# First norm with tokens as rows, x in four transfers, weight products moved behind the router product

## The reference

```python
x = x + 0.5 * L0_ffn(layernorm(x), Wg, W_in, W_out)   # 8 experts, top 2 with capacity, gelu(a) * g
x = x + L0_attn(layernorm(x), ...)                    # 16 heads of 8, causal, ALiBi
x = x + 0.5 * L0_ffn(layernorm(x), ...)
x = x + 0.5 * L1_ffn(x, ...)                          # latent attention, rope, 8 experts + shared
x = x + L1_attn(x, ...)                               # convolution, scan, feed-forward
x = x + 0.5 * L1_ffn(x, ...)
```

## Time and profile before

| | us |
|---|---|
| median of 3 runs | 1422.37 (1421.27 to 1424.42) |
| the profiled execution | 1424.82 |
| its span, first to last instruction | 1423.0 |
| TensorE busy | 1323.8 (93%) |
| VectorE busy | 1005.4 (71%) |
| ScalarE busy | 871.2 (61%) |
| GpSimdE busy | 400.2 (28%) |
| mean granted TensorE clock | 0.981 |

### The profile page before, as it was taken

One profiled execution on the slowest core, in us unless ns is written; L12 is line 12 of the kernel. 1 busy time (PEld: TensorE's weight loads), 2 busy tenths in 40 slices (PEclk: granted clock), 3 DMA queues, 4 the chain that ended last, 5 costly groups with the idle time before them and its releaser, 6 DMA issues.

```text
span 1423.0 us, 27091 instructions
## 1 busy us (share of the span) xinstructions
PE 1323.8 (93%) x10934; PEld 562.0 (39%) x10934; DVE 1005.4 (71%) x1516; ACT 871.2 (61%) x1104; POOL 400.2 (28%) x331
## 2 busy tenths in 40 slices
PE   7999998889879999999999998989998999999997
PEld 5344333333324444333444343433433334433443
DVE  3534777889925347698887868688868697978735
ACT  3334347788784454276566767666768676675672
POOL 5554430110011755452220223022305033202010
PEclk8999999999999999999999999999999999999998
DMA  6633101000001731011111010110010101100100
GB/s 177 118 62 70 25 14 31 16 2 2 2 1 39 196 60 34 1 32 24 35 24 24 1 23 1 24 35 10 15 24 1 23 13 24 31 13 19 24 1 15
DMA packets 30291, 45.80 MB, mean 32 GB/s; under 512 B 5892, under 2 KB 10692, under 8 KB 30116
## 3 DMA queue, kind: packets, MB, share of 16 engines
q1 hardware_dynamic: 30168, 44.08, 14.0%
HBM read 25.39 MB, written 1.18 MB: 19 GB/s over the span
## 4 chain that ended last, share of the span: by engine, by line
PE 72%; DVE 11%; ACT 8%; issue 4%; SPq 3%; DMA 2%; POOL 0%; ACTq 0%; DVEq 0%
PE ps L1264 13%; PE ps L1364 11%; PE ps L1309 7%; ACT PR L1442 6%; PE ps L1230 5%; PE ps L1250 5%; PE ps L1231 5%; PE ps L1232 5%; DVE BM L1530 3%; PE ps L1844 3%; PE ps L1328 2%; PE ps L1242 2%; PE ps L1271 2%; PE ps L1375 2%; PE ps L1324 1%
## 5 line engine op out<-in xcount | busy, mean ns | idle before, releaser
L1442 ACT ACTIVATE PR<-ps 128x1024 f32<-128x1024 f32 x432 | 431.2, 1026 | 207.1 <-PE ps L1271 136.4
L1530 DVE TENSOR_REDUCE BM<-ps 128x2 f32<-128x1024 f32 (+2 forms) x384 | 350.4, 950 | 57.0 <-PE ps L1250 55.9
L1264 PE MATMUL ps<-QS,KS 48*128 48x512 f16 (+7 forms) x2688 | 306.1, 329 | 31.7 <-ACT PR L1442 22.5
L1364 PE MATMUL ps<-PR,VS 128*32 128x512 f32 (+3 forms) x2304 | 231.5, 499 | 2.2 <-ACT PR L1442 1.6
L1264 PEld LDWEIGHTS ps<-QS,KS 48*128 48x128 f16 (+1 forms) x2688 | 108.5, 95 | 203.6 <-ACT PR L1442 88.5
L1250 PE MATMUL ps<-KS,QS 48*128 48x128 f16 (+2 forms) x1728 | 161.7, 273 | 19.2 <-DVE BM L1530 10.8
L1523 DVE TENSOR_REDUCE BM<-ps 128x8 f32<-128x1024 f32 x96 | 116.8, 1220 | 39.3 <-PE ps L1250 38.5
L1250 PEld LDWEIGHTS ps<-KS,QS 48*128 48x128 f16 x1728 | 68.0, 94 | 135.3 <-issue 45.8
L1571 POOL TENSOR_TENSOR OS<-OS,RX 128x512 f32<-128x512 f32 x24 | 30.5, 1270 | 273.9 <-ACT RX L1458 273.9
L1230 PE MATMUL ps<-YA,QS 128*128 128x512 f16 x256 | 99.6, 389 | 0.8 <-DVE RX L1489 0.5
L1231 PE MATMUL ps<-YA,QS 128*128 128x512 f16 x256 | 99.2, 388 | 0.0
(11 more groups left out here) (299 smaller groups left out, 2054.9 us busy)
## 6 DMA issues: line engine op xcount, KB each, us to landing
PR<-gates SPq DMA_DIRECT2D x32, 512.0 KB, 12.5
QS<-KS SPq DMA_DIRECT2D x64, 128.0 KB
QS<-KS SPq DMA_DIRECT2D x64, 64.0 KB
WM<-W_in SPq DMA_DIRECT2D x1, 2048.0 KB, 9.0
QS<-HL SPq DMA_DIRECT2D x48, 32.0 KB
KS<-HL SPq DMA_DIRECT2D x48, 32.0 KB
QS<-CT SPq DMA_DIRECT2D x96, 2.0 KB
KS<-KS SPq DMA_DIRECT2D x8, 128.0 KB, 2.4
```

The costliest lines, as they stand in the source:

```text
L1264: ins = pe.matmul(ps[pair][:, w, off:off + cols], KS[rows, ks, kt * P:(kt + 1) * P], QS[rows, qs, (ph + 1) * TT - cols:(ph + 1) * TT], sta ...
L1364: ins = pe.matmul(dst[32 * j:32 * j + 32, TT - cols:TT], v, PR[:, buf, j, off:off + cols], start=(g == 0), stop=(g == NGRP[ph] - 1))
L1442: act.activation(dst, src, ACT.Exp, scale=0.125 if lat else 1.0).then_inc(sig["exp"], 1)
L1530: ins = dve.tensor_reduce(BM[:, ph, p, :, qt - 4 * ph, part], bnk[:, :, off:off + nk * P], AX.X, ALU.max)
```

## The change

x comes in four transfers of a quarter each, with a semaphore each, again token-major (`XR`). VectorE takes bn_stats and bn_aggr of each row (a token) and normalises with one tensor_scalar per 128 tokens, with mean and 1/std as scalars of the partition (`XS`). ScalarE computes 1/std for 4 x 128 tokens in one instruction of 128x4. TensorE turns x and the normalised rows, 16 tiles each; ScalarE copies both out of PSUM. The weight products leave the hand-written start and become two planner tasks `cmp` 0 and 1 on TensorE behind `rlg`, with priority 0. W_in and W_out are asked for earlier, only W_in is waited for before the experts begin, and the wait for all small weights moves from the front of TensorE's plan to the first down matmul.

```diff
-            "scl": 0.75, ... "cmc": 0.6}
+            "scl": 0.75, ... "cmc": 0.6, "cmp": 2.6}
...
-        if kind in ("rlg", "rrk", "rtp"):
+        if kind in ("rlg", "rrk", "rtp", "cmp"):
             return 0
...
-            x = add("DVE", "eh", ("eh", u), x, ("ed", u - self.NHE) if u >= self.NHE else None)
+            x = add("DVE", "eh", ("eh", u), x, ("ed", u - self.NHE) if u >= self.NHE else self.staged(u))
...
         self.router()
         for i in range(2):
-            self.add("ACT", "cm", ("cmc", i))
+            self.add("ACT", "cm", ("cmc", i), self.add("PE", "cm", ("cmp", i), ("rlg",)))
...
+    def staged(self, u):
+        return ("cmp", 1) if u >= 4 else None
...
-            sp.dma_start(PRf[:, 0:T].rearrange("p (i d) -> p i d", i=NTT),
-                         a["x"].rearrange("(i p) d -> p i d", p=P)).then_inc(s_x0, 16)
+            for t in range(NT):
+                sp.dma_start(XR[:, t, :, :], a["x"].rearrange("(t i p) d -> t p i d", p=P, t=NT)[t]).then_inc(s_x[t], 16)
             for dst, src in ((wqn, a["wqn"]), (wkb, a["wkb"]), (won[0], a["won"][:, 0:H // 2]),
-                             (won[1], a["won"][:, H // 2:H])):
+                             (won[1], a["won"][:, H // 2:H]), (w_rt0[:, :], a["Wg0"])):
                 sp.dma_start(dst, src).then_inc(s_wc, 16)
+            sp.dma_start(w_in, a["W_in"].rearrange("e p f -> p e f")).then_inc(s_wm, 16)
             loads = [
-                (w_rt0[:, :], a["Wg0"]), (wq0[:, :, :], ...),
+                (w_out, a["W_out"].rearrange("e (c p) o -> p e c o", p=P)), (wq0[:, :, :], ...),
...
-            load_moe_weights(sp)
...
         def pe_load(pe):
             pe.wait_ge(s_const, 1)
+            for t in range(NT):
+                pe.wait_ge(s_x[t], 16)
+                for i in range(4):
+                    ins = pe.transpose(bank(t)[:, i * P:(i + 1) * P], XR[:, t, i, :], identf[:, :])
+                ins.then_inc(s_ld, 1)
+            for t in range(NT):
+                pe.wait_ge(s_xc, t + 1)
+                pe.wait_ge(s_xup, t + 1)
+                for i in range(4):
+                    ins = pe.transpose(bank(t)[:, i * P:(i + 1) * P], XS[:, t, i, :], identf[:, :])
+                ins.then_inc(s_ld, 1)
 
         def dve_load(dve):
+            def stats(t):
+                dve.wait_ge(s_x[t], 16)
+                for i in range(4):
+                    ins = dve.bn_stats(STAT[:, t, i, :], XR[:, t, i, :])
+                ins.then_inc(s_mean, 1)
+                dve.wait_ge(s_mean, t + 1)
+                for i in range(4):
+                    ins = dve.bn_aggr(MV[:, t, i, :], STAT[:, t, i, :])
+                ins.then_inc(s_var, 1)
+            stats(0)
             for t in range(NT):
+                if t + 1 < NT:
+                    stats(t + 1)
+                dve.wait_ge(s_var, t + 1)
                 dve.wait_ge(s_rs, t + 1)
+                for i in range(4):
+                    ins = dve.tensor_scalar(XS[:, t, i, :], XR[:, t, i, :], MV[:, t, i, 0:1], RSTD[:, t, i:i + 1],
+                                            ALU.subtract, ALU.mult)
+                ins.then_inc(s_xc, 1)
+
+        def act_load(act):
             act.preload_act_table_set(LN_EXP)
+            act.wait_ge(s_const, 1)
             for t in range(NT):
                 act.wait_ge(s_var, t + 1)
+                act.activation(RSTD[:, t, :], MV[:, t, :, 1], ACT.Ln, bias=epsc[:, 0:1]).then_inc(s_va, 1)
+                act.wait_ge(s_va, t + 1)
+                act.activation(RSTD[:, t, :], RSTD[:, t, :], ACT.Exp, scale=-0.5).then_inc(s_rs, 1)
+                act.wait_ge(s_ld, t + 1)
+                act.copy(XT[:, tsl(t)], bank(t)).then_inc(s_xup, 1)
             for t in range(NT):
+                act.wait_ge(s_ld, NT + t + 1)
+                act.copy(XN[:, tsl(t)], bank(t)).then_inc(s_xn, 1)
...
             if kind == "rlg":
+                if not lat:
+                    pe.wait_ge(s_wc, 80)
...
                 if u >= plan.NHE:
                     dve.wait_ge(sig["ed"], c("ed", u - plan.NHE))
+                elif not lat and u >= 4:
+                    dve.wait_ge(sig["cmp"], 2)
...
+                elif kind == "cmp":
+                    i, = args
+                    for h in range(H):
+                        g, j = divmod(h, QUAD)
+                        if i == 0:
+                            ins = pe.matmul(bank(4)[:, h * 32:(h + 1) * 32], wqn[:, h, :], wkb[:, h, :], start=True, stop=True)
+                        else:
+                            ins = pe.matmul(bank(5)[32 * j:32 * j + 32, g * P:(g + 1) * P], wkb[:, h, :],
+                                            won[h // 8][:, h % 8, :], start=True, stop=True)
+                    ins.then_inc(sig["cmp"], 1)
                 else:
+                    if task == ("ed", 0):
+                        pe.wait_ge(s_w, N_WFIRST)
                     pe_attn(pe, False, c, plan, task)
...
-            act.wait_ge(s_wm, 32)
...
+                if task == ("ewh", 0):
+                    act.wait_ge(s_wm, 16)
...
             plan, c = plan_of(False), counter(False)
-            dve.wait_ge(s_wm, 32)
+            dve.wait_ge(s_wm, 16)
...
             pe_load(pe)
-            pe_norm(pe)
-            pe.wait_ge(s_w, N_WFIRST)
+            pe.wait_ge(s_const, N_CONST)
             pe_first(pe)
```

More of the change, by code:

```diff
@@ L321, in weights_ready @@
     def weights_ready(self, u):
+        return None
+    def staged(self, u):
         return None
@@ L779, in pr_part @@
             return PRf[:, o:o + n]
-        NSQ = pr_part(0, 2048).rearrange("p (a t) -> p a t", a=NT)
-        NRS = pr_part(2048, 2048).rearrange("p (a t) -> p a t", a=NT)
+        XR, XS = (pr_part(i * T, T).rearrange("p (t i d) -> p t i d", t=NT, i=4) for i in range(2))
+        STAT = pr_part(2 * T, 96).rearrange("p (t i c) -> p t i c", t=NT, i=4)
+        MV = pr_part(2 * T + 96, 32).rearrange("p (t i c) -> p t i c", t=NT, i=4)
+        RSTD = pr_part(2 * T + 128, 16).rearrange("p (t i) -> p t i", t=NT)
         GB = pr_part(0, 8192).rearrange("p (a e t) -> p a e t", a=2, e=E)
@@ L826, in build_program @@
         gate_d = nc.dram_tensor("gates", (4, E, T), F32, kind="Internal").ap()
-        s_x0 = sem("s_x0")
+        s_x = [sem(f"s_x{t}") for t in range(NT)]
         s_w = sem("s_w")
@@ L919, in pool_const @@
             ch.up(pool.memset(pick[:, :], 0.0))
+            ch.up(pool.memset(epsc[:, 0:1], EPS))
             ch.wait()
@@ L946, in pool_const @@
                 ins = pool.memset(desc[:, e:e + 1], float(E - e))
-            pool.memset(epsc[:, 0:1], EPS)
             ins = pool.memset(epsc[:, 1:2], EPS * EPS)
@@ L952, in pe_load @@
             pe.wait_ge(s_const, 1)
-            pe.wait_ge(s_x0, 16)
-            for i in range(NTT):
-                ins = pe.transpose(bank(i // 4)[:, (i % 4) * P:(i % 4 + 1) * P],
-                                   PRf[:, i * P:(i + 1) * P], identf[:, :])
-                if i % 4 == 3:
-                    ins.then_inc(s_ld, 1)
-        def dve_load(dve):
-            for t in range(NT):
-                dve.wait_ge(s_ld, t + 1)
-                dve.tensor_copy(XT[:, t * TT:(t + 1) * TT], bank(t)).then_inc(s_xup, 1)
@@ L973, in pe_comp @@
-        def pe_comp(pe, heads):
-            pe.wait_ge(s_wc, 64)
-            for h in heads:
-                ins = pe.matmul(bank(4)[:, h * 32:(h + 1) * 32], wqn[:, h, :], wkb[:, h, :], start=True, stop=True)
-            if h == H - 1:
-                ins.then_inc(s_comp, 1)
-        def pe_comp_out(pe):
-            for h in range(H):
-                g, j = divmod(h, QUAD)
-                ins = pe.matmul(bank(5)[32 * j:32 * j + 32, g * P:(g + 1) * P], wkb[:, h, :], won[h // 8][:, h % 8, :],
-                                start=True, stop=True)
-            ins.then_inc(s_comp, 1)
@@ L989, in pe_norm @@
-        def pe_norm(pe):
-            pe_comp(pe, range(0, 4))
-            pe.wait_ge(s_const, N_CONST)
-            pe.wait_ge(s_xup, NT)
-            for t in range(NT):
-                pe.matmul(bank(t), mean_w[:, :], XT[:, tsl(t)], start=True, stop=True).then_inc(s_mean, 1)
-            pe_comp(pe, range(4, 12))
-            for t in range(NT):
-                pe.wait_ge(s_sq, t + 1)
-                pe.matmul(bank(t), mean_w[:, :], NSQ[:, t, :], start=True, stop=True).then_inc(s_var, 1)
-            pe_comp(pe, range(12, H))
-            pe_comp_out(pe)
@@ L1002, in dve_norm @@
-        def dve_norm(dve):
-            for t in range(NT):
-                dve.wait_ge(s_mean, t + 1)
-                dve.tensor_tensor(XN[:, tsl(t)], XT[:, tsl(t)], bank(t), ALU.subtract).then_inc(s_xc, 1)
-            for t in range(NT):
-                dve.wait_ge(s_rs, t + 1)
-                dve.tensor_tensor(XN[:, tsl(t)], XN[:, tsl(t)], NRS[:, t, :], ALU.mult).then_inc(s_xn, 1)
-        def act_norm(act):
+            for t in range(NT):
[3 more added lines that the diff above has]
+                ins.then_inc(s_ld, 1)
```

(10 more changed lines are left out.)

20 lines of the change are left out of this document (7 added, 13 removed).

## The result

The changed kernel took 1430.16 us (median of 7 runs, 1427.12 to 1433.86) beside 1421.27 for the kernel before on the same chip: ratio 1.0048, 95% interval 1.0026 to 1.0070. Slower, where I forecast 1416.1, and outside the range of 1409 to 1421.5. Its profiled execution took 1427.12 us, with a span of 1425.4.

What follows compares the result with a forecast made beforehand. The bound was when TensorE's unbroken work begins: gates' transpose 5.8 us earlier (37.4 instead of 43.16) plus 0.5 from the clock gives 6.3. Median 1422.4 less 6.3 is 1416.1; 8-in-10 range 1409 to 1421.5.

Steps and rivals of the forecast that it cites:

- What bounds the start, and how the gain reaches the end: Kernel start: TensorE's chain bounds it; the gates' transpose at 43.16 us shifts, and its shift reaches the end one for one.
- x in four transfers: Load of x: first quarter lands near 4.1 us (bounds 3.6 and 7.7), the last at 7.7 as now.
- VectorE's prices: First norm: 0.26 us per bn_stats, 0.14 per bn_aggr, 0.26 per tensor_scalar; first quarter of XN at 14.6.
- its scaling 1.04: First norm on VectorE: the four tensor_scalar operations of a quarter take 1.04 us.
- rival 2: First norm: GpSimdE's memsets block VectorE's scalings, 12 of 16 waiting 0.46 us each; 1418.5, or 1420.8 with low-pace products; 20%.
- Rival 3: First norm: memsets block the statistics too, up to 11 us; router product end 32.2, transpose 48.4, time 1427; 7%.
- The products behind the router product: Weight products ahead of the rank matmuls: 5.0 to 9.6 us depending on clock level, middle 7.3 taken.
- From the rank matmuls to the transpose: 18 matmuls before the gates' transpose: 6.0 us, transpose at 37.4; first GpSimdE product 8.6 us after it.
- No change of the order: Planner's order of later work: everything shifts by nearly the same amount, no change counted; bounds 4 us either way.
- W_in, the later wait for the small weights: Weight loads: W_in there at 17, needed by 21; small weights' wait moves to the first down matmul near 48; no cost.
- the sum: Whole kernel: 6.3 us less, span 1416.7, profiled execution 1418.5, median 1416.1.

Runs made afterwards that it cites:

- clearing later: Changed kernel with one wait more: GpSimdE clears KS, QS and VS only after VectorE's last scaling; 1415.88 us, ratio 0.9960.
- norm only, clearing later: Changed kernel with the weight products back in the hand-written start and GpSimdE's clearing behind the normalised rows; 1416.04 us, ratio 0.9971.
- norm only: Changed kernel with the weight products back in the hand-written start, between the two sets of 16 turns; 1425.92 us, ratio 1.0023, unclear.
- gaps: Changed kernel with GpSimdE waits inside its clearing: behind each KS and QS memset 1419.08 us, only the eighth 1417.85, every fourth 1418.12 (one run each).
- two inputs: Changed kernel, clearing unmoved, scaling by scalar_tensor_tensor with 1/std as second tensor: 1417.01 us, ratio 0.9973; also with products behind the rank matmuls: 1417.72.
- products only: Kernel before, with only the weight products moved from the hand-written start to the plan behind the router product; 1424.48 us, ratio 1.0012, unclear.
- small memsets sooner: Changed kernel with GpSimdE's nine smallest memsets (128x1) made earlier, so the clearing directly follows a select; 1430.23 us, ratio 1.0062.

## Why the prediction was wrong, step by step

- **What bounds the start, and how the gain reaches the end.** Right for the start, and one for one only as far as the order is the same, up to 400 us. The transpose at 35.64 in place of 43.16 gave a shift of -8.3 at 60 us and -9.2 past 1000 with the clearing later; the transpose at 51.20 gave +7.2 at 60 in the changed kernel. Behind 436 us it moves even where the order is that of before: -5.9 from 60 to 400 us, -7.5 at 620 and -9.6 past 1000 (norm only, clearing later). No run shows why, and the executions of one kernel differ by more than that (the kernel before: 1416.68 to 1431.39 in 25 runs).
- **x in four transfers.** The first quarter landed at 3.8 (forecast 4.1), the last at 8.9 (7.7 "as now"; that was wrong, and cost nothing).
- **VectorE's prices.** Four statistics took 0.87 us, four aggregates 0.38, four undisturbed scalings 1.09, where I had 1.04, 0.56 and 1.04. Undisturbed, the router product began at 14.04 (forecast 14.6) and took 6.83 (6.6): its end at 20.9, forecast 21.2. That this agrees is in part luck, for the path was wrong. I let the router product begin with the first quarter of XN at 14.6 and found the fourth covered by 3 us; but all 16 turns of the normalised rows stand ahead of it in TensorE's queue, so it can begin only behind the last scaling and its turns. By my own figures that was 14.9 + 0.9 = 15.8. It began right behind the turns of 12.11 to 14.25 (records of matmuls in a row overlap), and as early as that only because the last scaling had ended at 13.08.
- **The step that failed: "its scaling 1.04".** One group took 13.71. I had the collision as rivals 2 and 3, and priced both by one rule: a wait for one memset, 0.46 us, at most once for each of the 24. That price came from a single row, an operation that had waited once for one GpSimdE instruction. The Trainium skill, page "SBUF — State Buffer", section "Who interferes with whom", says that whoever issues first has the ports for the whole instruction, and that the other is blocked; by it a wait ends with an instruction. The runs show that it need not: it ended with the next wait of the other engine, 13.2, 4.0 and 2.2 us on, as that wait was moved. The forecast should have had, for rival 2, an upper bound of the whole clearing, 22.1 less 9.2 = 12.9, because nothing in the trace of before excluded it: no operation of that form stands beside a memset there. With it the router product ends at 21.2 + 12.9 = 34.1; measured were 33.49, which is the undisturbed end of 20.87 and the 12.62 by which the group was longer (13.71 less 1.09).
- **Rival 3** had nearly the right size (router product end 32.2, transpose 48.4, 1427; measured 33.49, 51.20, 1430) by a wrong mechanism: the statistics were not blocked (0.86 us for four beside memsets, in the kernels with the two-input scaling and with gaps); they queued behind one blocked scaling. And its argument against, that the operation seen waiting had two inputs, pointed the wrong way: beside memsets the two-input form is the one that goes through. The Trainium skill, page "SBUF — State Buffer", section "Who interferes with whom", says that two inputs contend only with a GpSimdE operation that reads; the trace agrees (1.12 us for four beside memsets, 0.73 for one beside a select, and 1.62 for one of 128x512 beside GpSimdE's products).
- **The products behind the router product.** 7.3 forecast as the middle of 5.0 to 9.6; 8.8 in the changed kernel (35.99 to 44.81, all at the low pace) and 5.7 with the clearing later (23.38 to 29.11, the first 32 at the high one). Both paces occur, from one kernel to the next. In the sum the term was fair; but I had charged them against a norm that would be 11.5 us shorter. Where it was not, they were a pure loss of 5.6 us at 60 us (changed kernel against norm only), most of what the kernel had lost there.
- **From the rank matmuls to the transpose.** 6.0 forecast, 6.4 measured (44.81 to 51.20); the expert matmuls go from 0.43 us each to 0.22 at 49.5, 4.3 us behind the first of them at 45.21. First GpSimdE product 8.3 us behind the transpose (8.6 forecast).
- **"No change of the order".** Wrong: the written order differs at 202 of TensorE's places, nearly all in the first attention. In the profiles with the new order some 1 to 3 us are won between 200 and 400 us (products only: -0.2 to -3.0); with the old order the shift is constant there to 0.02 us (norm only). What of it is kept behind 436 can't be told, since the shift moves there with the old order as well. It lies inside my bound of 4. Between medians it isn't seen (1415.9 with the new order, 1416.0 with the old).
- **W_in, the later wait for the small weights.** W_in's landing took 11.6 us (9.0 before). In clearing later VectorE waited 3.0 us for it, until 16.1, well ahead of the router product's end, and TensorE began the first expert without a break: it cost nothing, as forecast.

In the five kernels in which the stall is gone (clearing later in three, two inputs in two) the time is 1415.9 to 1417.7, where 1416.1 was forecast: the time of the sum was met, and one collision was missing in it. That it was met so closely is in part luck. With the clearing later the transpose came at 35.64, forecast 37.4, and the shift at 60 us was -8.3, forecast -6.3, while the medians are 6.0 apart. The best versions are the changed kernel with the clearing behind the norm (1415.88) and the same with the products ahead (1416.04); both beat the kernel before by 0.3 to 0.4%, and one can't be told from the other.

## What to carry to other kernels

Before an operation of VectorE is swapped for a "faster" form, look at what GpSimdE does in the same microseconds; a run of its instructions without a wait can be, for that form, one block as long as the run, and this length belongs in the range. Constants and clearing that nobody needs yet go behind the critical start, or get a wait every few instructions to bound the stall. And a move that pays for itself only if another part of the change works should be priced once without that part.

## What the hardware showed that I had not expected

- A `tensor_scalar` of 128x128 fp32, both sides in SBUF, began just ahead of a run of memsets (0.51 us each, one every 0.46) and was kept out for 13.16 us, until GpSimdE's next semaphore wait; with that wait moved, 4.05 and 2.20 us. The memsets didn't slow down meanwhile (514 to 515 ns each).
- Once it had got in, the same pair took turns without any wait: two scalings and one memset in 0.61 us, the memsets at 0.67 and the scalings at 0.43 and 0.62.
- Not concerned: the statistics (0.86 for four), and `scalar_tensor_tensor` with two SBUF inputs (1.12 for four, against 1.09 for `tensor_scalar` alone); beside a select one of these took 0.73.
- The weight products ran at either pace at the same place, behind six expert matmuls of 0.43 us each: 32 in 3.94 us (clearing later) and 4.01 (small memsets sooner), or in 7.03 (the changed kernel, two inputs, products only). Where the record has both levels the pace goes with them: clearing later 1.00 from 23.8 to 27.2, products only 0.50 throughout. In the changed kernel and in two inputs 1.00 is recorded, but the expert matmuls ahead and behind took 0.43 us each, the pace of 0.50: in these stretches the pace tells the level and the record doesn't.
